# Grouped convolution with attention-like products: input planes made from one order of x, a fourth group's sums in two other PSUM banks, one copy moved ahead

## The chip, the cores and the metric

The kernel runs on one core of one Trainium2 chip. The metric is device microseconds of one execution, smaller is better. Three executions of the kernel before gave 394.09, 394.26 and 394.74 us (median 394.26 us). All arithmetic is float32.

## The reference

x is (8, 128, 64, 64): 8 images, 128 channels, 64 x 64 pixels. In short:

```
t1  = p1_w * x;  t2 = x + t1;  t4 = relu(x)
t5  = unfold(x, 3x7, pad 1,3)                    # 21 shifted copies of x per channel
t7  = p7_w @ t4                                  # 128x128 over channels
t12 = mean over 5 taps of (x - shifted t7)       # taps 3 apart along w
t10 = grouped 1x1 conv of t2 with p10_w (4 groups, 32 -> 21*32 channels)
t11 = t1 (c x 4096) @ t5^T / 64                  # never formed by the kernel
t13 = t11 @ t10 / sqrt(128*21)
out = max(t13, t12)
```

The kernel reorders the product: it convolves x with the 3x7 weights of each group (y), multiplies y by t1 over all pixels to a 128x128 matrix A, and then t13 = A @ t2.

## The kernel before

**Units.** An image's y is made in four groups of 32 channels; a group of an image is a unit u = 4 n + g, 32 units in all. The three rows of the weights are worked with a short transform along pairs of rows (four products for two rows of outputs). So a unit has four data planes, made by VectorE as sums or differences of rows of x (`V_0`, `V_2`, `V_1`, `V_3`), and weight planes `U_*`. On the 128 partitions lie 4 phases of the column by 32 channels. A unit's x comes in two orders of the phases: FRONT (1,2,3,4 or 2,1,4,3) and BACK, which is FRONT with its two halves of 64 partitions exchanged. `V_0` and `V_2` are made of FRONT, `V_1` and `V_3` of BACK, so that TensorE, which works as four 64x64 tiles, always has two different halves to run beside each other. Each order is one load of 561 KB (`load_group`, L186) into `xw[:, u % 3, order]`.

**Slots.** TensorE's order is written out by hand (L970 to L1043). For a unit u it computes planes 1 and 2 (`one_two(u, k)`, k = 0..2, then `single_taps(u)`), and planes 0 and 3 follow one slot later: ScalarE copies a bank (`copy_two`), VectorE combines the two banks (`seeds(u)`), the single taps of planes 0 and 3 come in `single_taps(u + 1)`, their dense part `zero_three(u, k)` in slot u + 2 for the first four units and one slot after u later on. Then VectorE transposes both banks into yT (`turn_y(u)`, L592). In this text slot u begins with `one_two(u, 0)`.

**Banks.** PSUM has eight banks: three sets of two for units (`ps_y[u % 3]`), `ps_p7` for the 5-tap product and `ps_t13` for A @ t2. Unit 3 uses unit 0's set, so `one_two(3, 0)` waits for `turn_y(0)` (L832), and units 4 and 5 wait likewise for `turn_y(1)` and `turn_y(2)`. A of image 0 goes to `ps_y[0][0]`, and unit 6 waits for ScalarE's copy of it, `scale_a(0)` (L390, L834).

**The other engines.** ScalarE's order (L395 to L515): `relu`, `seed_x` (writes x into a bank as the start of an accumulation), `base_half` (copies a finished 5-tap half out), `t2_half` (eight instructions), `copy_two`, `scale_a`. VectorE's: weight sums of groups 0 and 1, planes, seeds, transposes, box sums of relu(x), the final max. GpSimd makes the weight sums of groups 2 and 3 (`weights`, L281), the plane `V_3` of unit 1 (L295), and t1 (`t1_part`). SyncE issues all loads and stores in one order (L221 to L270); a load that waits holds all behind it. Near the start a load of x waits for the planes of the unit that used the buffer (L189 to L196).

**The end of the first image.** After slot 5's dense part, TensorE runs `pair_first/second(0, 0)` (5-tap halves 0 and 1), `y_times_t1(0)` (64 records, 7.4 us), `p7_whole(0, h)` for h = 2, 3, 4 and `single_taps(5)`; slot 6 follows, in which the 5-tap halves (0,5) and (0,6) and A @ t2 halves (0,0) and (0,1) are interleaved with units 6 and 5.

Of the kernel before, what the change touches and what calls it, by code (L numbers as in the profile page):

```python
# [60 lines left out]
def conv_seq_kernel(nc, x_nat, x_pix, x_conv, p1, p1T, p7T, w_tiles, out):  # L61
    with ExitStack() as ctx:
# [69 lines left out]
        outer_ready = sem("outer_ready")  # L132
        outer_later = sem("outer_later")
        single_done = sem("single_done")
# [35 lines left out]

        def inner(u, planes):

            return v_of(u)[:, planes, 1:1 + BLOCKS_IN, :]

# [7 lines left out]
        def _(sp):  # L182
# [3 lines left out]
            def load_group(u):  # L186
                if u >= UNITS:
                    return
                if u == 3:  # L189
                    sp.wait_ge(early_ready, 2)  # L190
                    sp.wait_ge(outer_ready, 2)
                elif u == 4:
                    sp.wait_ge(early_ready, 4)
                    sp.wait_ge(outer_later, 1)
                else:
                    wait(sp, v_ready, 3 * (u - 5) + 3)  # L196
                for order in range(2):
                    sp.dma_start(xw[:, u % 3, order], x_conv[u // GROUPS, u % GROUPS, order]).then_inc(  # L198
                        xw_loaded[u % 3][order], 16)
# [35 lines left out]
            load_pixels(0, 2, 4)  # L235
            load_natural(0, 1)
            load_natural(0, 2)
            load_group(5)
            load_natural(0, 3)
# [33 lines left out]
        def _(pool):  # L273
# [7 lines left out]
            def weights(g):  # L281
# [28 lines left out]
        def _(act):  # L310
# [13 lines left out]
            def copy_two(u):  # L324
                act.wait_ge(pq_done, u + 1)
                wait(act, seeded, 2 * u)
                copy(q_sb[:], ps_y[u % SETS][1][:], 0.5).then_inc(q_copied, 1)

# [10 lines left out]
            def seed_x(n, h):  # L339

                if n < 0:
                    return
                i = 8 * n + h
                act.wait_ge(xn_loaded[h // 2], 16 * (n + 1))
                act.wait_ge(p7_bank_set, WARM)
                if n == 0 and h < 5:
                    if h == 3:
                        act.wait_ge(y_turned, 2 * GROUPS)
                    elif h > 1:
                        act.wait_ge(base_ready, h // 2)  # L350
# [52 lines left out]
            swap(3)  # L403
            seed_x(0, 0)
            seed_x(0, 1)
            copy_two(2)
# [111 lines left out]
        def _(dve):  # L518
# [14 lines left out]
            def second_rows(b, order):  # L533

                return xw[:, b, order, 1, :, 0:PAIRS], xw[:, b, order, 1, :, 1:PAIRS + 1]

            def early_planes(u):

                dve.wait_ge(xw_loaded[u][FRONT], 16)
                x0, x2 = first_rows(u, FRONT)  # L540
                x1, _ = second_rows(u, FRONT)
                if u == 0:
                    nc.vector.tensor_tensor(inner(u, V_2), x1, x2, ALU.subtract).then_inc(early_ready, 1)
                else:
                    low(u, early_ready)
                dve.wait_ge(xw_loaded[u][BACK], 16)
                sum_plane(u, early_ready)

# [13 lines left out]
            def planes_low(u):  # L562
                if u >= UNITS:
                    return
                dve.wait_ge(xw_loaded[u % 3][FRONT], 16 * (u // 3 + 1))
                if u >= LATE:
                    dve.wait_ge(m_done, u - 2 - (u < LATE + 3))
                low(u, v_ready)

            def planes_high(u):  # L570

                if u >= UNITS:
                    return
                b = u % 3
                dve.wait_ge(xw_loaded[b][BACK], 16 * (u // 3 + 1))
                sum_plane(u, v_ready)
                x1, x3 = second_rows(b, BACK)
                nc.vector.tensor_tensor(inner(u, V_3), x3, x1, ALU.subtract).then_inc(v_ready, 1)

            def seeds(u):  # L580

                one, two = ps_y[u % SETS]
                dve.wait_ge(pq_done, u + 1)
# [8 lines left out]
            def turn_y(u):  # L592
# [5 lines left out]
                for e in range(2):  # L598
                    nc.vector.transpose(yT[:, e, :, CG * g:CG * (g + 1)], ps_y[u % SETS][e][:].rearrange(  # L599
                        "p (j r) -> p j r", r=PAIRS)).then_inc(y_turned, 1)  # L600
# [45 lines left out]
            early_planes(1)  # L646
            x0, x2 = first_rows(0, FRONT)
            nc.vector.tensor_tensor(inner(0, V_0), x0, x2, ALU.subtract).then_inc(outer_ready, 1)
            x1, x3 = second_rows(0, BACK)
            nc.vector.tensor_tensor(inner(0, V_3), x3, x1, ALU.subtract).then_inc(outer_ready, 1)  # L650
            seeds(0)
            planes_low(2)
            planes_high(2)

            seeds(1)
            planes_low(3)
            planes_high(3)
            turn_y(0)

            seeds(2)  # L660
            planes_low(4)
            planes_high(4)
# [109 lines left out]
        def _(pe):  # L772
# [40 lines left out]
            def planes_12(u):  # L813
                one, two = ps_y[u % SETS]
                return (two, U_2, V_2), (one, U_1, V_1)

            def planes_03(u):
                even, odd = ps_y[u % SETS]
                return (even, U_0, V_0), (odd, U_3, V_3)

            def one_two(u, k):

                if k == 0:
                    if u == 0:
                        pe.wait_ge(edges_zeroed, 2)
                    if u < 2:
                        pe.wait_ge(early_ready, 2 * u + 2)
                    else:
                        pe.wait_ge(v_ready, 3 * (u - 2) + 2)
                    if u < GROUPS:  # L830
                        pe.wait_ge(u_swapped, 2 * u + 2)
                    wait(pe, y_turned, 2 * (u - SETS) + 2)  # L832
                    if u % GROUPS == 2:
                        wait(pe, aT_ready, u // GROUPS)  # L834
                    if u == 6:
# [9 lines left out]
            def outer_planes(u):  # L845

                pe.wait_ge(seeded, 2 * u + 2)
                if u == 0:
                    pe.wait_ge(outer_ready, 2)
                elif u == 1:  # L850
                    pe.wait_ge(early_ready, 4)
                    pe.wait_ge(outer_later, 1)
                else:
                    pe.wait_ge(v_ready, 3 * (u - 2) + 3)

# [245 lines left out]
```

## Time and profile before

| | us |
|---|---|
| median of three runs | 394.26 |
| the profiled execution | 394.36 |
| its span, first to last instruction | 392.6 |
| TensorE busy | 382.3 (97%) |
| VectorE busy | 328.4 (84%) |
| ScalarE busy | 253.8 (65%) |
| GpSimd busy | 91.0 (23%) |
| DMA queue of loads and stores | 64.1% of 16 engines |

The profiled execution is 1.76 us longer than its span. All times of rows are counted from the span's start. A row of the timeline merges instructions of one line that follow each other: start, duration, engine, line, operation, output and inputs, count, and in brackets the idle time before with what ended it. One matrix product is two records. A Tensor record's start is what orders it; successive ones overlap. For an instruction that begins before its predecessor's record has ended (VectorE, ScalarE), the distance of two starts is the cost. The granted TensorE clock was 0.999 of full speed in the whole execution.

### The profile page before, as it was taken

Reading aid. Unit: us, or ns where it says so; the run is one execution under the profiler, and the core shown is the slowest. Engines: PE = TensorE matmul, PEld = TensorE weight load, DVE = VectorE, ACT = ScalarE, POOL = GpSimd, SP = SyncE. Lnnn points to the kernel's source line nnn. Section 1 sums busy time; section 2 is a strip of 40 time slices with the busy share of each in tenths; the row PEclk is TensorE's granted clock in tenths of the full one; section 3 lists DMA queues with packets and bytes.
Section 4 is the critical chain, followed back from the end, with each engine's and each line's share of the span. In section 5 each row is a group of like instructions: output and inputs, shape, how many; then the busy total and the mean of one; then the engine's idle time right before and its main releaser. Section 6 shows DMA issues by size and latency. Waiting matters only on the chain.

```text
span 392.6 us, 10225 instructions
## 1 busy us (share of the span) xinstructions
PE 382.3 (97%) x4022; PEld 174.5 (44%) x4022; DVE 328.4 (84%) x394; ACT 253.8 (65%) x721; POOL 91.0 (23%) x78
## 2 busy tenths in 40 slices
PE   6899998999999999999999999999999999999996
PEld 3233475433733347333563337433373333732383
DVE  6986998999798896888968889688868889688645
ACT  2444178778577683776646774667727768277790
POOL 1724400622022222222022220222202222122300
PEclk9999999999999999999999999999999999999999
DMA  8999017884877847776567846779377783463115
GB/s 306 396 406 408 17 57 276 336 296 154 293 248 251 298 149 239 278 253 226 198 217 253 303 146 216 221 261 335 122 256 230 252 314 107 152 202 107 56 56 214
DMA packets 28848, 89.37 MB, mean 228 GB/s; under 512 B 3328, under 2 KB 3840, under 8 KB 28800
## 3 DMA queue, kind: packets, MB, share of 16 engines
q1 hardware_dynamic: 28800, 88.72, 64.1%
q8 instruction: 32, 0.52, 0.5%
q14 instruction: 16, 0.13, 0.1%
HBM read 71.93 MB, written 16.78 MB: 226 GB/s over the span
## 4 chain that ended last, share of the span: by engine, by line
PE 93%; DVE 3%; DMA 2%; SPq 1%; issue 0%; DVEq 0%
PE ps_y L787 42%; PE ps_y L888 15%; PE ps_t L809 12%; PE ps_p L809 12%; PE ps_y L798 8%; DMA xw<-x_conv 2%; PE ps_y L1035 1%; DVE yT L599 1%; PE ps_y L809 1%; DVE v_planes L553 1%; DVE v_planes L559 0%; SPq L198 0%; PE ps_p L938 0%; PE ps_y L938 0%; PE ps_t L938 0%
## 5 line engine op out<-in xcount | busy, mean ns | idle before, releaser
L787 PE MATMUL ps_y<-v_planes,u_planes 64*64 64x512 f32 x1488 | 185.2, 594 | 4.4 <-DVE yT L599 1.8
L278 POOL TENSOR_TENSOR t1T<-t1T,p1T_sb 128x512 f32<-128x512 f32 x64 | 82.6, 1312 | 269.1 <-PE ps_y L798 216.4
L386 ACT ACTIVATE t<-xn,p_plus 128x64 f32<-128x64 f32 x512 | 128.0, 334 | 0.0
L809 PE MATMUL ps_t<-t,aT 64*64 64x512 f32 x440 | 113.3, 590 | 0.1
L809 PE MATMUL ps_p<-box,p_fifth 64*64 64x512 f32 x432 | 111.1, 589 | 0.0
L787 PEld LDWEIGHTS ps_y<-v_planes,u_planes 64*64 64x64 f32 x1488 | 58.4, 133 | 112.7 <-issue 105.4
L599 DVE STREAM_TRANSPOSE yT<-ps_y 128x512 f32<-128x512 f32 x64 | 42.0, 695 | 32.5 <-PE ps_y L798 30.3
L312 ACT ACTIVATE base<-ps_p 128x512 f32<-128x512 f32 x56 | 33.4, 596 | 54.5 <-PE ps_p L809 52.0
L888 PEld LDWEIGHTS ps_y<-t1T,yT 128*128 128x128 f32 x512 | 57.8, 192 | 6.5 <-issue 6.5
L888 PE MATMUL ps_y<-t1T,yT 128*128 128x128 f32 x512 | 59.3, 277 | 0.0
L633 DVE TENSOR_TENSOR base<-ps_t,base 128x512 f32<-128x512 f32 x56 | 38.4, 686 | 11.6 <-PE ps_t L809 11.3
L809 PEld LDWEIGHTS ps_t<-t,aT 64*64 64x64 f32 x440 | 31.3, 133 | 29.7 <-PE ps_t L809 14.5
L809 PEld LDWEIGHTS ps_p<-box,p_fifth 64*64 64x64 f32 x432 | 31.2, 133 | 26.4 <-issue 22.8
L609 DVE TENSOR_TENSOR pair_sum<-relu_pad 128x1120 f32<-128x1120 f32 x32 | 42.2, 1318 | 0.3 <-ACT relu_pad L335 0.3
L617 DVE TENSOR_TENSOR box<-pair_sum 128x1024 f32<-128x1024 f32 x32 | 41.0, 1281 | 0.6
L626 DVE TENSOR_TENSOR box<-box,relu_pad 128x1024 f32<-128x1024 f32 x32 | 39.9, 1247 | 0.4
L553 DVE TENSOR_TENSOR v_planes<-xw 128x1088 f32<-128x1088 f32 x30 | 39.4, 1313 | 0.8 <-DMA xw<-x_conv 0.8
L798 PE MATMUL ps_y<-v_planes,u_planes 32*32 32x512 f32 x992 | 38.3, 599 | 0.2
L312 ACT ACTIVATE ps_p<-xn 128x512 f32<-128x512 f32 x56 | 33.6, 601 | 6.0
L335 ACT ACTIVATE relu_pad<-xn 128x1024 f32<-128x1024 f32 x32 | 33.7, 1054 | 5.4 <-DVE box L626 5.4
L312 ACT ACTIVATE q_sb<-ps_y 128x512 f32<-128x512 f32 x32 | 18.7, 586 | 18.7 <-PE ps_y L798 18.7
L586 DVE SCALAR_TENSOR_TENSOR ps_y<-ps_y,q_sb 128x512 f32<-128x512 f32 x32 | 21.6, 674 | 3.5 <-ACT q_sb L312 3.5
(66 smaller groups left out, 167.4 us busy)
## 6 DMA issues: line engine op xcount, KB each, us to landing
xw<-x_conv SPq DMA_DIRECT2D x64, 561.0 KB, 6.7
xn<-x_nat SPq DMA_DIRECT2D x32, 512.0 KB, 4.5
t1T<-x_pix SPq DMA_DIRECT2D x32, 512.0 KB, 5.2
out<-base SPq DMA_DIRECT2D x63, 256.0 KB, 4.8
u_planes<-w_tiles SPq DMA_DIRECT2D x4, 336.0 KB, 7.0
out<-base SPq DMA_DIRECT2D x2, 128.0 KB, 2.0
p1T_sb<-p1T SPq DMA_DIRECT2D x1, 128.0 KB, 8.7
p_sb<-p7T SPq DMA_DIRECT2D x1, 64.0 KB, 8.3
```

Of the source, the lines that this page charges most:

```text
L278: nc.gpsimd.tensor_tensor(part, part, p1T_sb[:, e, :].unsqueeze(1).broadcast_to([P, 4, C]), ALU.mult).then_inc(t1_ready, 1)
L312: return nc.scalar.activation(dst, src, ACT.Copy, scale=scale)
L386: last = nc.scalar.activation(t2[:, h, W * r:W * (r + 1)], xn[:, f, at:at + W], ACT.Copy, scale=p1_plus[:, 8 * h + r:8 * h + r + 1])
L553: nc.vector.tensor_tensor(inner(u, slice(V_0, V_2 + 1)), xw[:, b, FRONT, :, :, 0:PAIRS], second, ALU.subtract).then_inc(ready, 1)
L599: nc.vector.transpose(yT[:, e, :, CG * g:CG * (g + 1)], ps_y[u % SETS][e][:].rearrange("p (j r) -> p j r", r=PAIRS)).then_inc(y_turned, 1)
L609: nc.vector.tensor_tensor(pair_sum[:], r[:, :, 0:PS_W], r[:, :, 3:3 + PS_W], ALU.add).then_inc(box_steps, 1)
L617: nc.vector.tensor_tensor(box[:, f, :].rearrange("p (a b) -> p a b", b=W), pair_sum[:, :, 0:W], pair_sum[:, :, 6:6 + W], ALU.add).then_inc ...
L626: nc.vector.tensor_tensor(dst, dst, relu_pad[:, i % 2, :, 12:12 + W], ALU.add).then_inc(box_steps, 1)
L787: last = nc.tensor.matmul(dst[TILE * pair:TILE * pair + TILE, :], weights_of(rows_of(half), u, weights, TILE * k, TILE), data_of(rows_of(h ...
L798: last = nc.tensor.matmul(dst[SMALL_TILE * to:SMALL_TILE * to + SMALL_TILE, :], weights_of(rows, u, weights, 3 * TILE, SMALL_TILE), data_o ...
L809: last = nc.tensor.matmul(dst[cols, 0:data.shape[-1]], weights[rows, cols], data[rows, :], start=start, stop=False, skip_group_check=True)
L888: last = nc.tensor.matmul(a_bank(n)[:, 0:P], yT[:, e, j, :], t1T[:, e, j, :], start=t == 0, stop=t == 2 * BLOCKS - 1)
```

## The change

Four things are changed, all in the first seven or so units; the steady part of the program is as before.

1. Units 0 and 1 (`TURNED = 2`) load only FRONT. Their `V_1` and `V_3` are made from FRONT by two VectorE instructions of 64 partitions each, which read one half of the partitions and write the other. GpSimd no longer makes `V_3` of unit 1.
2. Unit 3 uses `ps_p7` and `ps_t13` as its set; the other units before 4 use `ps_y[(u + 1) % 3]`. Units 4, 5, 6 wait for the transposes of units 0, 1, 2. The 5-tap halves 0 to 3 of image 0 use `ps_y[0]`, half 4 uses `ps_p7`, A of image 0 goes to `ps_t13`; unit 6 no longer waits for the copy of A.
3. In VectorE's order `V_0` and `V_3` of units 0 to 3 (`outer_planes`) stand behind later work. Loads 3 to 6 of x wait for both pairs of planes of the unit three before; load 5 is issued before natural part 2.
4. In ScalarE's order the first two `seed_x` follow `copy_two(4)`, `scale_a(0)` comes before `base_half(0, 2)`, and `t2_half(0, 3)` after `relu(1, 0)`.

```diff
-        early_p7 = {1: ps_t13, 3: ps_y[0][1], 4: ps_t13}
+        ps_fourth = [ps_p7, ps_t13]
+        early_p7 = {0: ps_y[0][0], 1: ps_y[0][1], 2: ps_y[0][0], 3: ps_y[0][1]}
...
+        def set_of(u):
+            if u == LATE - 1:
+                return ps_fourth
+            return ps_y[(u + 1 if u < LATE else u) % SETS]
         def a_bank(n):
-            return ps_y[(GROUPS * (n + 1) + 2) % SETS][0]
+            return ps_t13 if n == 0 else set_of(GROUPS * (n + 1) + 2)[0]
...
+        def pairs_done(u):
+            return 2 * (u + 1) + min(u + 1, TURNED)
...
             def load_group(u):
-                if u == 3:
-                    sp.wait_ge(early_ready, 2)
-                    sp.wait_ge(outer_ready, 2)
-                elif u == 4:
-                    sp.wait_ge(early_ready, 4)
-                    sp.wait_ge(outer_later, 1)
-                else:
-                    wait(sp, v_ready, 3 * (u - 5) + 3)
-                for order in range(2):
+                if 3 <= u < LATE + 3:
+                    sp.wait_ge(early_ready, pairs_done(u - 3))
+                    sp.wait_ge(outer_ready, pairs_done(u - 3))
+                elif u > 3:
+                    sp.wait_ge(v_ready, 3 * (u - 3 - LATE) + 3)
+                for order in range(1 if u < TURNED else 2):
...
-            pool.wait_ge(early_ready, 4)
+            pool.wait_ge(early_ready, pairs_done(1))
             weights(2)
-            nc.gpsimd.tensor_tensor(inner(1, V_3), ...).then_inc(outer_later, 1)
             weights(3)
...
+            def pair_of_planes(u, front, back, combine, ready):
+                b = u % 3
+                dve.wait_ge(xw_loaded[b][FRONT], 16 * loads(u, FRONT))
+                nc.vector.tensor_tensor(inner(u, front), ..., ALU.subtract).then_inc(ready, 1)
+                if u < TURNED:
+                    for half in range(2):
+                        to, at = (slice(TILE * k, TILE * k + TILE) for k in (half, 1 - half))
+                        first, second = combine(b, FRONT)
+                        nc.vector.tensor_tensor(inner(u, back, to), first[at], second[at],
+                                                ALU.add if back == V_1 else ALU.subtract).then_inc(ready, 1)
+                else:
+                    dve.wait_ge(xw_loaded[b][BACK], 16 * loads(u, BACK))
+                    ...
```

VectorE's order at the start, before and after:

```
before: weights(0) early(0) weights(1) early(1) V_0(0) V_3(0) seeds(0) planes(2) seeds(1) planes(3)
        turn_y(0) seeds(2) planes(4) turn_y(1) seeds(3) planes(5) turn_y(2) seeds(4) ...
after:  weights(0) early(0) weights(1) early(1) outer(0) seeds(0) early(2) seeds(1) outer(1) early(3)
        outer(2) turn_y(0) seeds(2) outer(3) planes(4) turn_y(1) seeds(3) planes(5) turn_y(2) seeds(4) ...
```

Here `early` is `V_2` and `V_1`, `outer` is `V_0` and `V_3`, and `planes` all four. (Before, `early(1)` made `V_0` as well.) ScalarE's order from slot 4's copy on:

```diff
-            seed_x(0, 0); seed_x(0, 1)          # these two stood before copy_two(2)
             copy_two(4)
+            seed_x(0, 0)
+            seed_x(0, 1)
             relu(0, 2)
             base_half(0, 0)
             seed_x(0, 2)
+            base_half(0, 1)
             seed_x(0, 3)
-            base_half(0, 1)
             seed_x(0, 4)
             t2_half(0, 2)
             relu(0, 3)
+            scale_a(0)
             base_half(0, 2)
             base_half(0, 3)
-            t2_half(0, 3)
-            scale_a(0)
             base_half(0, 4)
             seed_x(0, 5)
             copy_two(5)
             relu(1, 0)
+            t2_half(0, 3)
             t2_half(0, 4)
             base_half(0, 5)
             seed_x(0, 6)
```

## Rows read from the trace of the kernel before

**Rows 1.** The page's chain that ended last, shares of the span by engine.

```profile
PE 93%; DVE 3%; DMA 2%; SPq 1%; issue 0%; DVEq 0%
```

**Rows 2.** Timeline of TensorE, slots 0 to 3 (columns as told above).

```profile
11.41 1.09 PE L798 MATMUL ps_y<-v_planes,u_planes 32*32 32x512 f32 x16
12.43 3.12 PE L787 MATMUL ps_y<-v_planes,u_planes 64*64 64x512 f32 x24
15.64 1.27 PE L798 MATMUL ps_y<-v_planes,u_planes 32*32 32x512 f32 x32
18.07 5.38 PE L787 MATMUL ps_y<-v_planes,u_planes 64*64 64x512 f32 x48 [1.16 <-DVE v_planes L559]
23.38 1.22 PE L798 MATMUL ps_y<-v_planes,u_planes 32*32 32x512 f32 x32
24.99 1.09 PE L787 MATMUL ps_y<-base,u_planes 64*64 64x512 f32 x8 [0.39 <-DVE yT L599]
```

**Rows 3.** Timeline of TensorE, end of slot 5, begins of slots 6, 8 and 9.

```profile
57.39 1.02 PE L938 MATMUL ps_t<-box,p_fifth 128*128 128x512 f32 x2
58.34 1.14 PE L798 MATMUL ps_y<-v_planes,u_planes 32*32 32x512 f32 x32
60.51 1.09 PE L787 MATMUL ps_y<-v_planes,u_planes 64*64 64x512 f32 x8 [1.02 <-DVE yT L599]
...
80.83 1.11 PE L787 MATMUL ps_y<-v_planes,u_planes 64*64 64x512 f32 x8
...
90.69 1.10 PE L787 MATMUL ps_y<-v_planes,u_planes 64*64 64x512 f32 x8
```

**Rows 4.** Timeline of VectorE, 5 to 17 us.

```profile
5.49 0.73 DVE L543 TENSOR_TENSOR v_planes<-xw 128x544 f32<-128x544 f32 x1 [0.66 <-DMA xw<-x_conv]
7.38 0.73 DVE L559 TENSOR_TENSOR v_planes<-xw 128x544 f32<-128x544 f32 x1 [1.16 <-DMA xw<-x_conv]
8.22 0.39 DVE L523 TENSOR_TENSOR u_planes<-u_planes 128x224 f32<-128x224 f32 x1
9.62 1.29 DVE L553 TENSOR_TENSOR v_planes<-xw 128x1088 f32<-128x1088 f32 x1 [0.16 <-DMA xw<-x_conv]
11.64 0.72 DVE L648 TENSOR_TENSOR v_planes<-xw 128x544 f32<-128x544 f32 x1
12.28 1.18 DVE L650 TENSOR_TENSOR v_planes<-xw 128x544 f32<-128x544 f32 x1
14.71 2.20 DVE L553 TENSOR_TENSOR v_planes<-xw 128x1088 f32<-128x1088 f32 x1
```

**Rows 5.** Timeline of GpSimd, first weight sum of group 3.

```profile
16.25 1.18 POOL L285 TENSOR_TENSOR u_planes<-u_planes 128x224 f32<-128x224 f32 x1 [0.48 <-DMA u_planes<-w_tiles]
```

**Rows 6.** Timeline of ScalarE around the first copy of A.

```profile
59.99 0.26 ACT L312 ACTIVATE aT<-ps_y 128x128 f32<-128x128 f32 x1
60.15 0.58 ACT L312 ACTIVATE base<-ps_t 128x512 f32<-128x512 f32 x1
...
62.81 2.00 ACT L386 ACTIVATE t<-xn,p_plus 128x64 f32<-128x64 f32 x8
64.71 0.58 ACT L312 ACTIVATE base<-ps_p 128x512 f32<-128x512 f32 x1
65.41 0.60 ACT L312 ACTIVATE ps_p<-xn 128x512 f32<-128x512 f32 x1
```

**Rows 7.** Timeline of TensorE's weight loads: 5-tap half (0,6) in slot 6.

```profile
66.33 0.17 PEld L809 LDWEIGHTS ps_p<-box,p_fifth 64*64 64x64 f32 x2
```

**Rows 8.** Timeline of VectorE: box sum of part 2; max of half (0,1).

```profile
55.27 1.23 DVE L626 TENSOR_TENSOR box<-box,relu_pad 128x1024 f32<-128x1024 f32 x1
...
71.06 0.68 DVE L633 TENSOR_TENSOR base<-ps_t,base 128x512 f32<-128x512 f32 x1
```

**Rows 9.** DMA issues, 50 to 64 us: count, size, median us from issue to landing.

```profile
xw<-x_conv SPq DMA_DIRECT2D x2, 561.0 KB, 5.7
```

**Rows 10.** The same view, 13 to 30 us.

```profile
xw<-x_conv SPq DMA_DIRECT2D x10, 561.0 KB, 12.4
```

More of the change, by code:

```diff
@@ L32 @@
 LATE = 4
+TURNED = 2
 SMALL = 16 * 3
@@ L169, in v_of, with inner, loads @@
             return v_planes[:, u if u < LATE else (u + 2) % 3]
-        def inner(u, planes):
-            return v_of(u)[:, planes, 1:1 + BLOCKS_IN, :]
+        def inner(u, planes, rows=slice(0, P)):
+            return v_of(u)[rows, planes, 1:1 + BLOCKS_IN, :]
+        def pairs_done(u):
+            return 2 * (u + 1) + min(u + 1, TURNED)
+        def loads(u, order):
+            return u // 3 + 1 - (order == BACK and u % 3 < TURNED)
         def wait(eng, s, value):
@@ L326, in copy_two @@
                 wait(act, seeded, 2 * u)
-                copy(q_sb[:], ps_y[u % SETS][1][:], 0.5).then_inc(q_copied, 1)
+                copy(q_sb[:], set_of(u)[1][:], 0.5).then_inc(q_copied, 1)
             def relu(n, f):
@@ L403, in _ @@
             swap(3)
-            seed_x(0, 0)
-            seed_x(0, 1)
             copy_two(2)
@@ L535, in second_rows, with outer_planes @@
                 return xw[:, b, order, 1, :, 0:PAIRS], xw[:, b, order, 1, :, 1:PAIRS + 1]
-            def early_planes(u):
[L539 to L547, printed above, removed]
+            def pair_of_planes(u, front, back, combine, ready):
+                b = u % 3
+                dve.wait_ge(xw_loaded[b][FRONT], 16 * loads(u, FRONT))
+                nc.vector.tensor_tensor(inner(u, front), xw[:, b, FRONT, front == V_2, :, 0:PAIRS],
+                                        first_rows(b, FRONT)[1], ALU.subtract).then_inc(ready, 1)
+                if u < TURNED:
[4 more added lines that the diff above has]
+                                                ALU.add if back == V_1 else ALU.subtract).then_inc(ready, 1)
+                else:
+                    dve.wait_ge(xw_loaded[b][BACK], 16 * loads(u, BACK))
+                    first, second = combine(b, BACK)
+                    nc.vector.tensor_tensor(inner(u, back), first, second,
+                                            ALU.add if back == V_1 else ALU.subtract).then_inc(ready, 1)
+            def early_planes(u):
+                pair_of_planes(u, V_2, V_1, lambda b, order: (second_rows(b, order)[0], first_rows(b, order)[1]),
+                               early_ready)
+            def outer_planes(u):
+                pair_of_planes(u, V_0, V_3, lambda b, order: second_rows(b, order)[::-1], outer_ready)
             def low(u, ready):
@@ L564, in planes_low @@
                     return
-                dve.wait_ge(xw_loaded[u % 3][FRONT], 16 * (u // 3 + 1))
-                if u >= LATE:
-                    dve.wait_ge(m_done, u - 2 - (u < LATE + 3))
+                dve.wait_ge(xw_loaded[u % 3][FRONT], 16 * loads(u, FRONT))
+                dve.wait_ge(m_done, u - 2 - (u < LATE + 3))
                 low(u, v_ready)
@@ L574, in planes_high @@
                 b = u % 3
-                dve.wait_ge(xw_loaded[b][BACK], 16 * (u // 3 + 1))
+                dve.wait_ge(xw_loaded[b][BACK], 16 * loads(u, BACK))
                 sum_plane(u, v_ready)
@@ L580, in seeds @@
             def seeds(u):
-                one, two = ps_y[u % SETS]
+                one, two = set_of(u)
                 dve.wait_ge(pq_done, u + 1)
@@ L598, in turn_y @@
                 for e in range(2):
-                    nc.vector.transpose(yT[:, e, :, CG * g:CG * (g + 1)], ps_y[u % SETS][e][:].rearrange(
+                    nc.vector.transpose(yT[:, e, :, CG * g:CG * (g + 1)], set_of(u)[e][:].rearrange(
                         "p (j r) -> p j r", r=PAIRS)).then_inc(y_turned, 1)
@@ L646, in _ @@
             early_planes(1)
[L647 to L650, printed above, removed]
+            outer_planes(0)
             seeds(0)
-            planes_low(2)
-            planes_high(2)
+            early_planes(2)
             seeds(1)
-            planes_low(3)
-            planes_high(3)
+            outer_planes(1)
+            early_planes(3)
+            outer_planes(2)
             turn_y(0)
             seeds(2)
+            outer_planes(3)
             planes_low(4)
@@ L813, in planes_12 @@
             def planes_12(u):
-                one, two = ps_y[u % SETS]
+                one, two = set_of(u)
                 return (two, U_2, V_2), (one, U_1, V_1)
             def planes_03(u):
-                even, odd = ps_y[u % SETS]
+                even, odd = set_of(u)
                 return (even, U_0, V_0), (odd, U_3, V_3)
```

36 lines of the change are left out of this document (15 added, 21 removed).

## The prediction

> **What bounds the kernel now.** I read the page first, then the chain of waits, then the timeline of each engine for the first 90 us. The chain runs 93% over TensorE [rows 1]: all that can be won is time in which TensorE stands. After slot 8 it hardly does: slot 8 lasts 90.69 - 80.83 = 9.86 us with nothing waited for [rows 3]. So I measure every step by when TensorE reaches a mark, and what is won at 80.83 us is won at the end. Four places are visible before that mark. (a) The first product waits for planes 1 and 2 of unit 0, whose second one begins at 7.38 us, released by a load [rows 4]. (b) Slot 2 begins at 18.07, released by VectorE's planes; the single taps before it began at 15.64 [rows 2]. (c) Slots 3, 4 and 5 wait for a transpose: from single taps to the next slot 24.99 - 23.38 = 1.61 us [rows 2]; the trace repeats the pattern twice, at the begins of slots 4 and 5. (d) Slot 6 begins 60.51 - 58.34 = 2.17 us after its single taps [rows 3]. The bracket names a transpose, but unit 6's bank set was long transposed; what ended just then is ScalarE's copy of A, 59.99 + 0.26 = 60.25 [rows 6]. What that distance is without a wait I take from the turn of slots 0 and 1, 12.43 - 11.41 = 1.02 [rows 2], plus 0.05 for twice the taps: 1.07 us.
>
> **The first planes (one load less).** The distance of two starts of a 544-column instruction on VectorE is 12.28 - 11.64 = 0.64 [rows 4]. What 64 partitions that read one half and write the other cost, no row shows. Bounds: below, half of 0.64, if cost went by elements; above, the 1.18 of the slowed instruction at 12.28 [rows 4]. I take 0.64, since the instruction has the same 544 columns. Then: V_2 at 5.49 (FRONT's landing is not later than before), halves of V_1 at 6.13 and 6.77, end 7.50 instead of 7.38 + 0.73 = 8.11. TensorE starts 0.61 earlier, at 7.6.
> Weight sums of group 1: 8.22 to 9.46 before (9.62 less 0.16 of idle), start to start 1.28 with the next instruction; now 7.41 to 8.69. Planes of unit 1: x FRONT landed at 9.6 with the BACK load of unit 0 ahead of it, which cost 7.38 - 5.49 = 1.89; now it lands by 7.7 to 8.2, before 8.69. Three instructions of 0.64: early(1) is complete at 10.70. TensorE's own pace is slower: with 3.21 us of dense (15.64 - 12.43 [rows 2]) and the 1.02 slot 1 is at 7.60 + 3.21 + 1.02 = 11.83, its single taps at 15.04, and slot 2 could begin at 15.04 + 1.07 = 16.11.
>
> **Slot 2 is still VectorE's.** outer(0): V_0 at 10.61; V_3 in two halves from 11.25. GpSimd's weight sums start when early(1) is done, so from 10.9 they run beside these. A 544-column instruction beside them takes 1.18, next start 1.10 later (the one at 12.28 [rows 4]). The two halves: 11.25, 12.35, seeds at 13.45. From 12.28 to 14.71 before lie one such instruction and two seeds [rows 4], so seeds are 1.33: they end the stretch at 14.78 (the single taps of plane 0/3 at 15.04 have them by 0.15). early(2), still beside GpSimd, whose group 3 sums now come at once because their load is 3.3 us earlier: V_2 at 14.78, V_1 at 15.88, end 17.06. Slot 2 at 17.12 instead of 18.07: gain 0.95, with 1.0 us of stall left. Bounds of this step: with halves at 0.32 the planes would no longer bind much and the gain is 2.5; with all four halves ahead of slot 1 at 1.18 VectorE is 4 x 0.54 = 2.2 later, slot 2 at 19.3, a loss of 1.2.
> Here the trace shows how the two engines meet: the 1088-column instruction at 14.71 took 2.20, where that at 9.62 took 1.29 [rows 4], and GpSimd's sum begun at 16.25 ended at 17.43, 0.52 after VectorE's 16.91 [rows 5]. The Trainium skill (SBUF — State Buffer, "Who interferes with whom") says that a VectorE instruction with two SBUF inputs and a GpSimd one that reads SBUF exclude each other for a whole instruction. The rows agree, and it speaks against the change: each extra instruction is one more opening for GpSimd. Without the rule, at 0.64 each, slot 2 would begin at TensorE's own 16.11 and the kernel end 1.0 earlier than I say.
>
> **Slots 3, 4, 5 (the fourth bank set).** Slot 2's dense part takes 23.38 - 18.07 = 5.31 [rows 2]: single taps at 22.43. Unit 3 has no transpose to wait for: slot 3 at 23.50, slot 4 at 29.88, slot 5 at 36.26 (6.38 each). What could be late instead: turn_y(0) now stands behind early(3) and outer(2) but is wanted at 29.88; it ends near 24.1. early(3) ends at 17.0 + 1.4 (seeds) + 1.9 (outer(1)) + 1.3 = 21.6 against 23.50. outer(3) ends at 26.9 and planes(4) at 28.8 against 29.88. So three times 1.61 - 1.07 = 0.54 goes: 1.62, and the gain at slot 5 is 2.57.
>
> **Loads.** Load 4 of x now waits for outer(1), 20.3 us; all behind it on SyncE's queue (pixels 2 and 3, natural 1, loads 5, 6) waits too. The loads ahead of it are 1.15 MB less and are landing by then, so the queue is nearly quiet: from a quiet queue a load lands in 5.7 [rows 9], 26.1 against planes(4) at 26.9. Load 5 lands near 32, planes(5) done near 34 against 36.26. I put this at nothing; its price if wrong is in the third rival.
>
> **The end of image 0.** The box sum of part 2 is shifted with seeds(4), which follow slot 4's single taps: these are now at 29.88 + 5.31 = 35.19, before at 23.38 + 2 x (5.31 + 1.61) = 37.22, so by 2.03; TensorE by 2.57 from slot 5 on. It ended at 55.27 + 1.23 = 56.50 and was wanted at 57.39 [rows 8, 3]; now 54.47 and 54.82. Still covered; if not, it costs up to 0.5. Single taps of slot 5: 58.34 - 2.56 = 55.78. Without the wait for A, slot 6 at 56.85 instead of 60.51: a further 1.10, 3.66 in all.
> **Most of that comes back at once.** ScalarE is busy without a gap from base_half(0,4), which follows p7_whole(0,4) (57.39 + 1.02 and a little for the signal = 58.45 before, 55.89 now [rows 3]), to seed_x(0,6). Before, that run was 60.15 to 65.41 + 0.60 = 66.01, 5.86 us [rows 6]. Now t2_half(0,3) stands in it, 64.71 - 62.81 = 1.90 more [rows 6]: 55.89 + 7.76 = 63.65. TensorE wants it for half (0,6), at 66.33 - 60.51 = 5.82 after the slot's start [rows 7, 3], at 62.67. It stands 1.05 and goes on at 63.72 instead of 66.33: gain 2.61.
> From 66.33 to 80.83 are 14.50 us; unhindered it would be 4.23 + 9.86 = 14.09 (4.23 is slot 8's own tail). Of the 0.41 lost, 0.3 is in slot 7, where max of half (0,1) began only at 71.06 [rows 8], behind a box sum slowed by GpSimd's first t1 part. Pixels of image 1 are issued behind natural(1,1), which waits for t2_half(0,3) (60.45, as before in absolute time), so this meeting falls 2.6 us later against TensorE, where VectorE has room: 0.3 to 0.4 more. Bounds: 0 to 0.41.
>
> **Sum.** 0.95 + 1.62 + 1.10 - 1.05 + 0.35 = 2.97. From the profiled execution, 394.36 (span 392.6, 1.76 around it), that gives 391.4, and against the median 394.26, 0.1 lower, 391.3 us.
>
> **Rivals.** One: ScalarE doesn't bind in slot 6, for instance because the copies are ready sooner than I chain them. For it: it had idle stretches before 56 us. Against: the run is gapless and starts from TensorE's own product. The 1.05 stays won: 390.3.
> Two: VectorE's start is dearer than I price it (halves above 0.64, GpSimd in one opening more), and slot 2 stays where it was. For it: no row shows such an instruction, and four are ahead of slot 1. Against: same columns. Without the 0.95: 392.3; at the upper bound, 2.2 lost of 2.97: 393.5.
> Three, slower than before: load 4, held until outer(1), meets a busy queue. Its place is planes(4) in front of slot 4. Planes 1 and 2 follow FRONT's landing by 2.0, so slot 4 = landing + 2.0; it decides from 29.88 + 2.97 - 2.0 = 30.9, a landing 10.5 after the issue at 20.4. At the 12.4 that loads took in a busy queue [rows 10] slot 4 begins at 34.8, 4.9 late: 396.2. For it: 12.4 was the rule in just this stretch. Against: those loads were issued far ahead, into a queue that this wait drains.
>
> **Chances.** Forecast (391.3, own spread 390.9 to 391.8) 0.52; first rival 0.13; second 0.22; third 0.05; the rest 0.08, mostly small stalls of the tight places (0.15 for seeds(0), 0.4 for the box sum) that give 391.8 to 392.3. The range 390.2 to 392.7 takes in the first rival and the middle of the second. A run can tell 0.2% (0.8 us) from no change; below 393.5 is faster: 0.90, same 0.05, slower 0.05.
>
> **What would show it.** First product at 7.6, slot 2 near 17.1 released by VectorE; no idle at slots 3 to 5, slot 5 near 36.3; slot 6 near 56.9; then an idle of about 1 us of TensorE before a 5-tap product, released by ScalarE, near 62.7 to 63.7; slot 8 near 77.9. It is wrong if the 64-partition instructions take other than 0.73, if a plane of units 4 or 5 shows idle before it from a load beyond 1 us, or if slot 6 runs through.

## The result and the profile after

The changed kernel took 395.94 us (median of six runs, 394.43 to 396.70) against 394.11 for the kernel before (also six runs): ratio 1.0047, 95% interval 1.0035 to 1.0059. It is slower by 0.5%, outside the range 390.2 to 392.7 that I gave, and on the other side. The three longest of the six, 396.4 to 396.7, have a mean TensorE clock of 0.996 of full speed; the other three, at 1.000, took 394.4 to 395.5.

The profiled execution is the fastest of the six (394.43, span 392.7), so its trace shows the smallest form of the loss. First TensorE's timeline, the marks that answer to those of before: slots 2, 3 and 4; single taps and slot 6; the two places where it waits for ScalarE; slots 8 and 9. (L811 is the dense product, L822 the single taps, L833 the 5-tap and A @ t2 halves.)

```profile
17.59 5.38 PE L811 MATMUL ps_y<-v_planes,u_planes 64*64 64x512 f32 x48 [0.93 <-DVE v_planes L564]
...
24.05 0.64 PE L811 MATMUL ps_t<-base,u_planes 64*64 64x512 f32 x1
...
30.52 5.38 PE L811 MATMUL ps_y<-v_planes,u_planes 64*64 64x512 f32 x48
...
56.50 1.14 PE L822 MATMUL ps_y<-v_planes,u_planes 32*32 32x512 f32 x32
57.57 1.11 PE L811 MATMUL ps_y<-v_planes,u_planes 64*64 64x512 f32 x8
...
64.53 0.65 PE L833 MATMUL ps_p<-box,p_fifth 64*64 64x512 f32 x2 [0.71 <-ACT ps_p L322]
...
78.32 1.09 PE L811 MATMUL ps_y<-v_planes,u_planes 64*64 64x512 f32 x8
81.26 0.65 PE L833 MATMUL ps_p<-box,p_fifth 64*64 64x512 f32 x2 [1.84 <-ACT ps_p L322]
...
90.32 1.11 PE L811 MATMUL ps_y<-v_planes,u_planes 64*64 64x512 f32 x8
```

The waits at slots 3 to 5 are gone, single taps and slot 6 are 1.07 apart instead of 2.17, and at slot 8 TensorE is 2.51 us ahead of [rows 3] (78.32 against 80.83). In slot 8 it loses nearly all: 90.32 - 78.32 = 12.00 us against 9.86, and slot 9 begins 0.37 ahead. (That this trace is ahead at all comes from the start of the one before, which was about 0.7 later than in two other kernels with the same start, e3 and e6 below.) From there the two traces run in parallel until 363 us, where the last 0.36 goes at a wait for VectorE's seeds of the last unit, whose cause I did not find.

The wait in slot 8 is for a seed, which stands behind `base_half(1,0)` on ScalarE. That copy overwrites the half (0,0) of the output and must wait for its store. ScalarE's timeline, and SyncE's, after:

```profile
79.80 0.60 ACT L322 ACTIVATE base<-ps_p 128x512 f32<-128x512 f32 x1 [4.32 <-DMA out<-base]
```

```profile
48.60 13.03 SPq L216 DMA_DIRECT2D xn<-x_nat  x2
61.69 0.91 SPq L210 DMA_DIRECT2D xw<-x_conv  x2
62.64 2.23 SPq L225 DMA_DIRECT2D t1T<-x_pix  x4
66.36 0.33 SPq L216 DMA_DIRECT2D xn<-x_nat  x1
66.73 0.92 SPq L210 DMA_DIRECT2D xw<-x_conv  x2
67.69 1.75 SPq L231 DMA_DIRECT2D out<-base  x2
```

The first line merges two loads of natural x; the second of them, natural(1,1), waits for `t2_half(0,3)`, and everything stands behind it. Load 8 of x follows at 61.69; before, it went at 60.50, while TensorE was 2.2 to 2.9 us later. Load 8, four pixel loads, natural(1,2) and load 9, nine transfers, then go in one stretch ahead of the store. The issues view of the store's moment, changed kernel and kernel before:

```profile
out<-base SPq DMA_DIRECT2D x1, 256.0 KB, 12.0
```

```profile
out<-base SPq DMA_DIRECT2D x1, 256.0 KB, 8.9
```

Issued at 67.69 it landed at 79.7, and ScalarE had stood 4.32 us. Before, issued at 69.30, it landed at 78.2, ahead of its use at 79.86. So the store was issued earlier than before and landed later: what makes it late is how much still travels in front of it. The pixels are late too (GpSimd's t1 parts of image 1 begin at 70.54 instead of 68.55), and they meet VectorE's planes. VectorE's timeline, planes of unit 8:

```profile
73.42 1.76 DVE L580 TENSOR_TENSOR v_planes<-xw 128x1088 f32<-128x1088 f32 x1
75.11 1.80 DVE L586 TENSOR_TENSOR v_planes<-xw 128x544 f32<-128x544 f32 x1
76.83 1.80 DVE L604 TENSOR_TENSOR v_planes<-xw 128x544 f32<-128x544 f32 x1
```

### The profile page after: what moved, and what is told of

The parts are those of the page before. It is cut to its first block, busy times and chain, and to the rows that moved or that the text cites. A ratio compares the mean times of both kernels' runs of the same rounds, so it can differ in the third digit from the quotient of the medians.

```text
span 392.7 us, 10231 instructions
## 1 busy us (share of the span) xinstructions
PE 383.0 (98%) x4022; PEld 172.6 (44%) x4022; DVE 333.4 (85%) x402; ACT 254.0 (65%) x721; POOL 92.4 (24%) x77
## 4 chain that ended last, share of the span: by engine, by line
PE 83%; DVE 8%; DMA 4%; ACT 2%; issue 1%; DVEq 0%; SPq 0%; ACTq 0%
PE ps_y L811 37%; PE ps_y L910 13%; PE ps_t L833 11%; PE ps_p L833 11%; PE ps_y L822 8%; DMA out<-base 3%; DVE pair_sum L635 2%; PE ps_y L1055 1%; DVE box L643 1%; DMA xw<-x_conv 1%; DVE v_planes L559 1%; ACT t L398 1%; DVE v_planes L553 1%; PE ps_y L833 1%; DVE ps_y L612 1%
## 5 line engine op out<-in xcount | busy, mean ns | idle before, releaser
L811 PE MATMUL ps_y<-v_planes,u_planes 64*64 64x512 f32 x1488 | 184.3, 595 | 1.5 <-DVE v_planes L564 0.9
L290 POOL TENSOR_TENSOR t1T<-t1T,p1T_sb 128x512 f32<-128x512 f32 x64 | 84.9, 1349 | 269.0 <-PE ps_y L822 211.7
L833 PE MATMUL ps_t<-t,aT 64*64 64x512 f32 x440 | 113.3, 590 | 0.1
L833 PE MATMUL ps_p<-box,p_fifth 64*64 64x512 f32 x424 | 109.1, 590 | 2.6 <-ACT ps_p L322 2.6
L811 PEld LDWEIGHTS ps_y<-v_planes,u_planes 64*64 64x64 f32 x1488 | 57.1, 133 | 111.8 <-issue 103.8
L625 DVE STREAM_TRANSPOSE yT<-ps_y 128x512 f32<-128x512 f32 x62 | 40.7, 694 | 30.5 <-PE ps_y L822 30.1
L910 PEld LDWEIGHTS ps_y<-t1T,yT 128*128 128x128 f32 x448 | 50.6, 192 | 5.7 <-issue 5.7
L910 PE MATMUL ps_y<-t1T,yT 128*128 128x128 f32 x448 | 51.9, 277 | 0.0
L833 PEld LDWEIGHTS ps_t<-t,aT 64*64 64x64 f32 x440 | 31.4, 133 | 29.7 <-PE ps_t L833 14.7
L635 DVE TENSOR_TENSOR pair_sum<-relu_pad 128x1120 f32<-128x1120 f32 x32 | 43.3, 1352 | 0.3 <-ACT relu_pad L345 0.3
L833 PEld LDWEIGHTS ps_p<-box,p_fifth 64*64 64x64 f32 x424 | 30.5, 133 | 28.8 <-issue 26.1
L643 DVE TENSOR_TENSOR box<-pair_sum 128x1024 f32<-128x1024 f32 x32 | 39.1, 1222 | 0.6
L822 PE MATMUL ps_y<-v_planes,u_planes 32*32 32x512 f32 x992 | 38.3, 599 | 0.2
L580 DVE TENSOR_TENSOR v_planes<-xw 128x1088 f32<-128x1088 f32 x28 | 36.4, 1299 | 0.1
L322 ACT ACTIVATE aT<-ps_y 128x128 f32<-128x128 f32 x6 | 1.7, 277 | 33.1 <-PE ps_y L910 33.1
```

The costliest lines, as they stand in the source:

```text
L290: nc.gpsimd.tensor_tensor(part, part, p1T_sb[:, e, :].unsqueeze(1).broadcast_to([P, 4, C]), ALU.mult).then_inc(t1_ready, 1)
L322: return nc.scalar.activation(dst, src, ACT.Copy, scale=scale)
L625: nc.vector.transpose(yT[:, e, :, CG * g:CG * (g + 1)], set_of(u)[e][:].rearrange("p (j r) -> p j r", r=PAIRS)).then_inc(y_turned, 1)
L635: nc.vector.tensor_tensor(pair_sum[:], r[:, :, 0:PS_W], r[:, :, 3:3 + PS_W], ALU.add).then_inc(box_steps, 1)
L643: nc.vector.tensor_tensor(box[:, f, :].rearrange("p (a b) -> p a b", b=W), pair_sum[:, :, 0:W], pair_sum[:, :, 6:6 + W], ALU.add).then_inc ...
L811: last = nc.tensor.matmul(dst[TILE * pair:TILE * pair + TILE, :], weights_of(rows_of(half), u, weights, TILE * k, TILE), data_of(rows_of(h ...
```

## The experiments

Each stands against the kernel before, measured with it: medians 393.79 (e1 to e4), 393.91 (e6 to e9) and 393.78 (e10 to e13). `e1` is the change with one call moved, and is the base of several others.

**e1: t2_half(0,3) in an idle stretch.**

```diff
             seed_x(0, 1)
+            t2_half(0, 3)
             relu(0, 2)
...
             relu(1, 0)
-            t2_half(0, 3)
             t2_half(0, 4)
```

> The changed kernel, but ScalarE's t2_half(0,3) stands in its idle stretch after the first two seeds (38.6 to 43.0 us) instead of behind relu(1,0). Theory (the gain is lost at the store): the changed kernel's TensorE waits 1.84 us in slot 8 for ScalarE's base_half(1,0), which waits for the store of half (0,0); that store's place in the load queue hangs on natural(1,1), which waits for t2_half(0,3), issued 61.3. Here natural(1,1) is issued near 56.5, the store lands by 76, no idle in slot 8, and the 0.71 of slot 6 goes too: slot 9 near 87.3 instead of 90.3, about 391.3 us, ratio near 0.993. Rival (the store wait covers another bound at the same place, VectorE's planes slowed by GpSimd to 1.8 us each): slot 9 not before 89.5, time 393.5 or more.

391.58 us (391.54 to 391.60 in five runs, one at 393.28), ratio 0.9951 (0.9939 to 0.9964). Load 8 goes at 56.57 instead of 61.69, no wait in slot 6 or slot 8, slot 9 at 87.5. SyncE's timeline:

```profile
48.38 8.14 SPq L216 DMA_DIRECT2D xn<-x_nat  x2
56.57 0.90 SPq L210 DMA_DIRECT2D xw<-x_conv  x2
57.51 2.22 SPq L225 DMA_DIRECT2D t1T<-x_pix  x4
```

The store, issued at 65.70, takes 8.9 us and lands at 74.6. One group of eight ScalarE instructions moved turns +0.5% into -0.5%. Why one run of six took 393.28 is open.

**e2: the store of (0,0) ahead of the pixels.**

```diff
+                if n == 1:
+                    store(0, 0)
                 load_pixels(n)
...
-                store(n - 1, 0)
+                if n > 1:
+                    store(n - 1, 0)
                 store(n - 1, 1)
```

> The changed kernel, but the store of half (0,0) is issued ahead of the pixels of image 1, everything else as it is. Theory: it lands by 69, slot 8 has no idle before its 5-tap product, the 0.71 of slot 6 stays: slot 9 near 88.2, the time 2 us below the changed kernel's, 392.3 to 393.5. Rival (VectorE is as late as the store): less than 0.7 us below the changed kernel's.

394.71 us, ratio 1.0025 (1.0015 to 1.0035): a gain over the changed kernel of about 1, between both expectations. The wait for the store is gone, another took its place. TensorE, GpSimd and VectorE:

```profile
81.26 0.65 PE L836 MATMUL ps_t<-t,aT 64*64 64x512 f32 x2 [1.05 <-DVE base L662]
```

```profile
72.22 10.65 POOL L293 TENSOR_TENSOR t1T<-t1T,p1T_sb 128x512 f32<-128x512 f32 x6 [26.99 <-DMA t1T<-x_pix]
```

```profile
72.99 1.77 DVE L583 TENSOR_TENSOR v_planes<-xw 128x1088 f32<-128x1088 f32 x1
74.68 1.80 DVE L589 TENSOR_TENSOR v_planes<-xw 128x544 f32<-128x544 f32 x1
76.40 1.80 DVE L607 TENSOR_TENSOR v_planes<-xw 128x544 f32<-128x544 f32 x1
78.12 2.39 DVE L638 TENSOR_TENSOR pair_sum<-relu_pad 128x1120 f32<-128x1120 f32 x1
```

The late queue has two effects of about the same lateness; the theory named one, and the rival the other. The pixels arrive late, six t1 parts run back to back, and the VectorE instructions with two SBUF inputs that meet them wait out most of one: 1.80 instead of 0.72 (the first, of 1088 columns, 1.77 instead of 1.28). The max of a half, which A @ t2 waits for, comes last. The Trainium skill (SBUF — State Buffer, "Who interferes with whom") says that the second input of such an instruction comes through a read interface shared with GpSimd, and that the shared ports are an exclusive lock. The trace agrees: 1.80 is 0.72 plus 1.08, most of a t1 part of 1.25.

**e3: ScalarE's part of the change alone, on the kernel before.**

```diff
             relu(0, 3)
+            scale_a(0)
             base_half(0, 2)
             base_half(0, 3)
-            t2_half(0, 3)
-            scale_a(0)
             base_half(0, 4)
...
             relu(1, 0)
+            t2_half(0, 3)
             t2_half(0, 4)
```

> The kernel before with ScalarE's part of the change alone: scale_a(0) ahead of base_half(0,2), t2_half(0,3) behind relu(1,0). Theory: slot 6 begins 1.1 earlier, about 1 comes back as a wait for the seed of (0,6), natural(1,1) is issued 3 to 4 us later (63.5 to 64), the store of (0,0) lands 3 later, near 81.5, and slot 8 waits 1.5 to 2.5: the time 1.3 to 2.5 above before, 395.4 to 396.6, ratio 1.003 to 1.006. Rival (the loss belongs to the bank sets or to the loads at the start): within 0.5 us of before.

396.51 us, ratio 1.0080 (1.0067 to 1.0093). The same two waits of TensorE, 0.71 and 1.72; ScalarE:

```profile
80.83 0.60 ACT L312 ACTIVATE base<-ps_p 128x512 f32<-128x512 f32 x1 [4.20 <-DMA out<-base]
```

Load 8 goes at 62.86. The edit carries the whole loss and more; the rest of the change wins some of it back.

**e6: the same with t2_half(0,3) early.** As e3, but `t2_half(0, 3)` stands ahead of `relu(0, 2)`.

> The kernel before, with scale_a(0) ahead of base_half(0,2) as in the change, but t2_half(0,3) moved forward into ScalarE's idle stretch before relu(0,2), not behind relu(1,0). Theory (the place of t2_half(0,3) alone makes the sign): slot 6 begins 1.1 earlier with no wait later, natural(1,1) is issued near 58.3 instead of 60.4: 1.0 to 1.5 us below before, 392.3 to 392.8. Rival (moving the copy of A ahead is itself what costs): no faster than before.

392.58 us, ratio 0.9970 (0.9960 to 0.9979). With both edits the kernel is 1.3 us below before. In the trace 1.10 of it is at slot 6 (58.73 - 57.66 = 1.07 after its single taps instead of 2.17), which is the earlier copy of A; the rest the run does not split.

**e8: only the place of one load.** ScalarE's order stays as changed.

```diff
-                load_natural(n, 1)
+                if n > 1:
+                    load_natural(n, 1)
                 load_group(u + 4)
                 store(n - 2, 6)
                 load_pixels(n)
+                if n == 1:
+                    load_natural(n, 1)
```

> The changed kernel with ScalarE's order as changed, and only the place of one load moved: natural(1,1), which waits for t2_half(0,3), is issued behind load 8 of x and the pixels of image 1 instead of ahead of them. Theory (the late queue is the whole loss, by the store and by GpSimd's late t1 parts): slot 8 has no wait, VectorE's planes in slot 7 are not slowed to 1.8 each; the 0.7 of slot 6 stays: 0.7 to 1.0 above e1, 392.2 to 392.7. Rival (ScalarE's order costs in slot 8 by itself): 394 or more.

392.08 us (391.96 to 392.25), ratio 0.9947 (0.9934 to 0.9960), just below the range. The rival, that ScalarE's order costs by itself, falls: the order costs its 0.7 in slot 6 and nothing in slot 8, and 3.9 of the changed kernel's us (medians; 2.3 between the profiled executions) were the head of SyncE's queue waiting. The store is issued at 67.53 here, as late as in the changed kernel (67.69), but load 8 and the pixels went 10 us earlier (48.71 and 51.36), and it lands after 6.7 us instead of 12.0:

```profile
out<-base SPq DMA_DIRECT2D x1, 256.0 KB, 6.7
```

**e4: no turned halves.** `TURNED = 0` in the changed kernel.

> The changed kernel with TURNED = 0: units 0 and 1 load both orders again, V_1 and V_3 made in one instruction each; banks, order and ScalarE's part as changed. Theory: first product 0.5 later, slot 2 at 17.9 to 18.1, so 0.3 to 0.5 of the gain at the start is gone, and since t2_half(0,3) and with it the queue behind natural(1,1) move along with TensorE, the end moves by the same: 0.3 to 0.5 above the changed kernel. Rival (the turned halves are what costs, by traffic between VectorE and GpSimd): faster than the changed kernel by 1 us or more.

396.29 us, but from 393.66 to 398.68 over twelve runs, ratio 1.0068 (1.0044 to 1.0092): from the changed kernel's 1.0047 (1.0035 to 1.0059) it can't be told apart. The time agrees with the expectation by luck, since slot 2 went the other way: it begins at 16.53, 1.06 earlier than with the turned halves. Two things move it. With fewer instructions VectorE reaches `early(2)` 0.95 earlier (14.41 against 15.36). And group 3's weights land later, GpSimd's sums of them miss `early(2)`, and its two planes take 0.72 each. The gain is lost again: a load makes the planes of unit 5 wait 1.33 us, and before the first 5-tap product TensorE waits 1.09 for a box sum. The changed kernel's, then this one's:

```profile
15.36 1.08 DVE L553 TENSOR_TENSOR v_planes<-xw 128x544 f32<-128x544 f32 x1
16.36 1.18 DVE L564 TENSOR_TENSOR v_planes<-xw 128x544 f32<-128x544 f32 x1
```

```profile
14.41 0.72 DVE L553 TENSOR_TENSOR v_planes<-xw 128x544 f32<-128x544 f32 x1
15.04 0.72 DVE L564 TENSOR_TENSOR v_planes<-xw 128x544 f32<-128x544 f32 x1
```

This trace also shows what a longer stand does. In slot 8 TensorE stood 2.20 us, and the granted clock fell (windows: us, then busy us and count of each engine, clock, DMA share, GB/s):

```profile
70.00:80.00 10.00, 9.75 (x112) 3.19 (x104) 9.97 (x9) 5.66 (x19) 8.53 (x5) 1.00 1.02 392
80.00:84.00 4.00, 2.05 (x10) 1.43 (x14) 3.98 (x5) 3.39 (x8) 2.71 (x2) 0.70 1.00 394
84.00:88.00 4.00, 4.00 (x38) 2.71 (x34) 3.95 (x5) 2.58 (x9) 0.00 (x0) 0.87 0.89 300
```

0.70 and 0.87 are averages of stretches at 2.4 GHz and at 1.2 GHz: over 82 to 84 us alone it is 0.50. Slot 8 lasts 92.59 - 78.66 = 13.93 us here, 1.93 more than in the changed kernel's trace; 0.36 of it is the longer wait, so about 1.6 (an estimate) is the price of the lower clock. The changed kernel's three runs at a mean clock of 0.996 have no trace, so that their clock fell at the same wait is inferred.

**e9: e1 without turned halves.**

> e1 with TURNED = 0: both orders loaded for units 0 and 1. Theory (first part of the change is worth little by itself: a load less, but two more VectorE instructions at 0.75): slot 2 about 1 earlier as seen with TURNED = 0 before, then a load of unit 5 late by 1.3 and about 1 us lost before the first 5-tap products: 391.3 to 392.3, with more spread than e1. Rival (the turned halves are a plain loss of 1 us): 390.6 or less, steady.

393.62 us, two runs at 390.65 and ten from 393.48 to 395.24, ratio 0.9981 (0.9961 to 1.0002). The profiled one is one of the two (390.67) and shows no wait after slot 0. The interval includes no change, and neither expectation had two levels.

**e7: e1 with group 3's sums after early(2).**

```diff
             weights(2)
+            pool.wait_ge(early_ready, pairs_done(2))
             weights(3)
```

> The kernel with t2_half(0,3) early (e1), and GpSimd's weight sums of group 3 held until early(2) is done, so that VectorE makes the planes of unit 2 alone. Theory (the two engines exclude each other for whole instructions): V_2 and V_1 of unit 2 take 0.72 instead of 1.08 and 1.18, slot 2 begins 0.8 earlier (16.5 to 16.7 instead of 17.4 to 17.6) and the end moves by 0.5 to 0.8: 390.8 to 391.1. Rival (what is won at slot 2 is lost again at the loads or at the box sum, as in the run without turned halves): within 0.3 of e1's 391.6.

396.24 us, 394.30 to 397.69, ratio 1.0045 (1.0025 to 1.0065): 4.7 slower than e1 although slot 2 came 0.8 earlier, as expected. Both expectations missed. The profiled execution, at full clock, is 2.9 slower (394.43 against 391.57), and that much the waits below explain: slot 6 begins at 60.20 against 57.34. Seven of the twelve runs have a mean clock of 0.991 to 0.996 and take 396.2 to 397.7, the five others 394.3 to 394.7. The rest of the 4.7 goes with the lower clock, where in those runs is not shown. VectorE in slots 2 to 4, and the wait that it gave TensorE:

```profile
22.77 1.80 DVE L565 TENSOR_TENSOR v_planes<-xw 128x544 f32<-128x544 f32 x1
...
29.50 1.78 DVE L587 TENSOR_TENSOR v_planes<-xw 128x544 f32<-128x544 f32 x1
31.21 1.79 DVE L605 TENSOR_TENSOR v_planes<-xw 128x544 f32<-128x544 f32 x1
...
37.29 1.80 DVE L605 TENSOR_TENSOR v_planes<-xw 128x544 f32<-128x544 f32 x1
```

```profile
31.34 5.38 PE L812 MATMUL ps_y<-v_planes,u_planes 64*64 64x512 f32 x48 [1.76 <-DVE v_planes L587]
...
46.38 1.19 PE L834 MATMUL ps_y<-box,p_fifth 64*64 64x512 f32 x8 [1.48 <-DVE box L653]
```

With TensorE earlier, the t1 parts, released by its `m_done` (the first by its load of pixels), begin among VectorE's planes instead of beside the transposes, and each hit costs about 1.08.

**e11, e12, e13: the t1 parts of image 0 paced.** Each pair starts only where VectorE turns to PSUM (transposes and seeds). e13 is e1 with it, e11 is e7 with it, e12 is e9 with it.

```diff
             for q in range(8):
                 pool.wait_ge(m_done, 1 + q // 2)
+                if q == 0:
+                    pool.wait_ge(outer_ready, pairs_done(2))
+                elif q in (2, 4):
+                    pool.wait_ge(v_ready, 3 * (q // 2))
+                elif q == 6:
+                    pool.wait_ge(box_steps, BOX_STEPS)
                 t1_part(0, q)
```

> The kernel e7 (t2_half(0,3) early, group 3's sums after early(2)) with GpSimd's t1 parts of image 0 started only where VectorE begins a transpose and seeds, which read PSUM: after outer(2), after the planes of units 4 and 5, after the first box sum. Theory (e7 lost its 4.7 us because GpSimd's 1.25 us parts fell in front of VectorE's planes, 1.08 us each time): no plane above 1.2 us, slot 2 at 16.6, no wait in slots 4 and 5: 390.6 to 391.2, and steady within 0.4. Rival (the loss of e7 is the load queue or something else): above 393 or spread over more than 2 us.

391.20 us (390.88 to 391.93), ratio 0.9929 (0.9914 to 0.9944): 5.0 below e7 by four waits more. Its spread of 1.0 is wider than I said, and pacing has a price here: TensorE waits 0.51 us for the last t1 part before A of image 0 (at 46.03).

> e9 (t2_half(0,3) early, no turned halves) with the same paced t1 parts. Theory: e9's twelve runs of 390.65 to 395.24 become steady near the fast ones, 390.5 to 391.2, since their spread is the race between VectorE and GpSimd. Rival (e9's spread comes from its later load of unit 5): spread stays above 2 us.

390.04 us (390.00 to 390.51 in four runs), ratio 0.9900 (0.9885 to 0.9916): the fastest version, 1.0% below the kernel before. The rival for e9's spread, the load of unit 5, falls: that load is still 0.77 late here, and TensorE does not wait for it. GpSimd's parts and VectorE's planes of units 4 and 5:

```profile
29.07 2.51 POOL L290 TENSOR_TENSOR t1T<-t1T,p1T_sb 128x512 f32<-128x512 f32 x2 [3.92 <-PE ps_y L817]
35.33 2.51 POOL L290 TENSOR_TENSOR t1T<-t1T,p1T_sb 128x512 f32<-128x512 f32 x2 [3.75 <-PE ps_y L817]
```

```profile
27.58 0.72 DVE L592 TENSOR_TENSOR v_planes<-xw 128x544 f32<-128x544 f32 x1
28.21 0.72 DVE L610 TENSOR_TENSOR v_planes<-xw 128x544 f32<-128x544 f32 x1
32.43 1.29 DVE L586 TENSOR_TENSOR v_planes<-xw 128x1088 f32<-128x1088 f32 x1 [0.77 <-DMA xw<-x_conv]
```

> e1 with the paced t1 parts alone. Theory: e1's common time is kept, 391.3 to 391.6, since its parts fell well already, and the one run in six at 393.3 goes. Rival (holding GpSimd makes the t1 parts late for A of image 0): above 392.

391.87 us, ratio 0.9949 (0.9934 to 0.9963), one run of six still at 393.01. It lies between the two expectations, 0.3 above e1, and the odd run stays: pacing gives nothing where the parts fell well, and the odd run has another cause, which stays open.

**e10: the waits for the transposes put back.** In e1, `one_two(u, 0)` for u = 3, 4, 5 also waits for `y_turned >= 2 * (u - 3) + 2`. (The edit also makes unit 6 wait for `turn_y(3)`, which costs nothing: slot 6 begins 1.07 after its single taps.)

> e1 with TensorE's waits for the transposes of units 0, 1, 2 put back in front of slots 3, 4, 5 (the other bank set stays in use, its freedom is taken away). Theory: with the queue behind natural(1,1) out of the way, TensorE's three waits of 0.5 are paid in full at the end: 1.4 to 1.9 above e1, 393.0 to 393.5. Rival (VectorE sets the pace through slot 5 anyway): less than 0.7 above e1.

393.48 us (393.33 to 393.66), ratio 0.9986 (0.9975 to 0.9996). In the changed order the fourth bank set is worth 1.9 us, once the gain can reach the end. The trace splits it: against e1 slots 3, 4 and 5 begin 0.98, 0.45 and 0.46 later after their single taps. The first is twice the others because `turn_y(0)` stands later in the changed order of VectorE; TensorE waits 0.92 for it, where the kernel before waited 0.39.

## Why the prediction was wrong

**The step that failed** is the one by which the sum stops at the start of slot 8: "After slot 8 it hardly does ... So I measure every step by when TensorE reaches a mark, and what is won at 80.83 us is won at the end." That put a wait in slot 8 at nothing, as in the trace before, where the transfers had been in time for a later TensorE. Measured, slot 8 lasts 12.00 us instead of 9.86, with 1.84 of TensorE's wait for a seed in it, and of 2.51 us won at its start 0.37 is left at slot 9.

The prediction had the cause in hand one step earlier: "Pixels of image 1 are issued behind natural(1,1), which waits for t2_half(0,3) (60.45, as before in absolute time), so this meeting falls 2.6 us later against TensorE, where VectorE has room: 0.3 to 0.4 more." The gain itself came, 0.32 in slot 7 (from 2.19 ahead to 2.51), but the same late queue took more than that in slot 8. It restarted even later than I said (load 8 at 61.69), VectorE had no room (e2), and I did not go down the queue: behind nine other transfers stands the store that ScalarE needs in slot 8. Before, that store had 1.7 us in hand (78.2 against 79.86). With TensorE 2.5 earlier and the store 1.5 later, that is a wait of about 2. e8 shows it by moving one load, e3 by causing the loss in the kernel before, e1 by removing the cause. My rivals had no such case: the one that ended slower than before was about load 4, for which nothing waited, and I followed SyncE's queue no further than 60 us.

**Point by point**, for the first planes: first product 7.6, measured 7.72. The two 64-partition halves took 1.47 together, 0.75 from start to start, not 0.64. VectorE's timeline, planes of unit 1 and the first of the next pair:

```profile
8.81 0.72 DVE L553 TENSOR_TENSOR v_planes<-xw 128x544 f32<-128x544 f32 x1
9.56 1.47 DVE L559 TENSOR_TENSOR v_planes<-xw 64x544 f32<-64x544 f32 x2
11.06 0.73 DVE L553 TENSOR_TENSOR v_planes<-xw 128x544 f32<-128x544 f32 x1
```

The terms of the sum, and what the two profiled executions give for them:

| | forecast | measured |
|---|---|---|
| slot 2 | 0.95 | 0.48 |
| slots 3, 4, 5 | 1.62 | 1.36 |
| wait for A at slot 6 | 1.10 | 1.10 |
| wait for the seed of (0,6) | -1.05 | -0.71 |
| from there to slot 8 | 0.35 | 0.28 |
| at slot 8 | 2.97 | 2.51 |
| slot 8 itself | 0 | -2.14 |

Slot 2 came at 17.59 instead of 17.12. And its gain was not the change's: the kernel before itself, with only ScalarE's order edited, begins slot 2 at 17.39 in e3 and in e6, because its load landed earlier than in the one profiled execution that I took as the standard (the plane that waits for it begins at 6.54 and 6.67, not at 7.38). The turned halves bring nothing to slot 2, and without them it begins at 16.5. At slots 3 to 5 the waits are gone as forecast, but the distance without a wait is 1.15 there (24.05 - 22.91, 30.52 - 29.37), not the 1.07 that I took from another turn; 1.07 is right at slot 6. The load of unit 4, my third rival: no wait of VectorE for it.

**What the sum left out besides:** the clock. The median is 1.5 above the profiled execution. The three runs with a mean clock of 0.996 are about 1 us longer than two at full clock (396.4 to 396.7 against 395.4 and 395.5); why those two are 1 us above the profiled one is open, for want of a trace.

## What to carry to other kernels

When an instruction is moved, follow each queue whose head waits for it to the end of what stands behind, stores included, and compare every landing with the new time of its use, not the old one. A gain on the bounding engine makes all transfers that are not tied to it later, against it, by as much. A single execution taken as the standard can carry the size of the effect sought. And price two engines that exclude each other by where their instructions will meet after the shift: pacing one of them to the other's PSUM work made the earlier start worth having.

## What was not expected of the hardware

- The same operation on 64 partitions that reads the other half costs 0.75 from start to start, where the 128-partition one costs 0.64: half the partitions save nothing. Whether the 0.11 more comes from the half or from the crossing, no run separates.
- A VectorE instruction of 0.72 us that met a GpSimd part of 1.25 took 1.78 to 1.81. A shift of 0.8 us upstream turned this from no plane hit by a t1 part of image 0 to four and cost 2.9 us between the profiled executions (e7 against e1), 4.7 between medians, with the runs of lower mean clock in them.
- TensorE idle for 1.84 us kept its clock in the profiled run of the change; idle for 2.20 in e4 it was granted 0.70 of 2.4 GHz over the 4 us that hold the idle time, and 0.87 over the next 4.
- A store of 256 KB issued at the same moment (67.5 to 67.7) took 12.0 us from issue to landing in the changed kernel and 6.7 in e8, where the loads ahead of it had gone 10 us earlier.
- First products of kernels with the same start began at 8.21, 7.37 and 7.56 us (before, e3, e6): a single profiled execution carries 0.8 us of that.
